# Adding up the scaled parts of a chunk with eight identity matmuls on TensorE, all input shares first, and the FFN half a chunk later

## The reference, cut to what matters

```python
# x: (32, 32, 256) = batch, time, features; cond: (32, 256) is the first state
# 1. a GRU over 32 time steps (state h: 32 x 256, weights 256 x 768)
gi = x_t @ W_ih + b_ih;  gh = h @ W_hh + b_hh
r = sigmoid(i_r + h_r);  z = sigmoid(i_z + h_z)
n = tanh(i_n + r * h_n); h = (1 - z) * n + z * h
# 2. an FFN over all 1024 states (tokens), a mixture of 128 experts on 8 basis parts of 128
probs = softmax(h @ w_router); top 4 -> topk_w (normed)
basis = silu(h @ w_gate) * (h @ w_up)            # 8 parts of 128
mix   = rows of (a0**2 + a1**2) / sum, per expert
out   = sum over the 4 of topk_w * scale * (mix_sel . basis) @ w_down
out  += silu(h @ sw_gate) * (h @ sw_up) @ sw_down  # the shared expert, 256 wide
# 3. result = x + out
```

## Time and profile before

| what | before |
|---|---|
| median of 3 runs | 151.68 us (151.32 to 153.98) |
| the profiled execution | 151.24 us, span of the trace 149.4 us |
| PE matmuls busy | 136.4 us (91%), 1482 records |
| PE weight loads busy | 99.2 us (66%) |
| DVE / ACT / POOL busy | 110.7 / 68.3 / 66.3 us |
| mean granted TensorE clock | 0.985 of full speed |

### The profile page before, as it was taken

One profiled execution on the slowest core, in us unless ns is written; L12 is line 12 of the kernel. 1 busy time (PEld: TensorE's weight loads), 2 busy tenths in 40 slices (PEclk: granted clock), 3 DMA queues, 4 the chain that ended last, 5 costly groups with the idle time before them and its releaser, 6 DMA issues.

```text
span 149.4 us, 4027 instructions
## 1 busy us (share of the span) xinstructions
PE 136.4 (91%) x1482; PEld 99.2 (66%) x1482; DVE 110.7 (74%) x410; ACT 68.3 (46%) x222; POOL 66.3 (44%) x125
## 2 busy tenths in 40 slices
PE   7939999799973998999999999999999999899991
PEld 5528877576552665866777676767766875588880
DVE  2113668699987499789878987898888789859661
ACT  1303466666436454544544554455544552513830
POOL 2201113477459197149324923481457146556030
PEclk9995999999999999999999999999999999999998
DMA  3999990000000000000000000100010001000102
GB/s 89 346 208 213 383 318 9 7 4 2 0 0 4 0 0 4 0 16 23 4 0 29 11 0 0 37 4 0 2 39 0 0 4 37 0 0 0 35 4 70
DMA packets 5763, 7.12 MB, mean 48 GB/s; under 512 B 880, under 2 KB 4208, under 8 KB 5744
## 3 DMA queue, kind: packets, MB, share of 16 engines
q1 hardware_dynamic: 5324, 6.63, 15.9%
q10 hardware_dynamic: 420, 0.24, 0.6%
HBM read 5.81 MB, written 1.05 MB: 46 GB/s over the span
## 4 chain that ended last, share of the span: by engine, by line
PE 68%; DVE 12%; POOL 6%; DMA 5%; ACT 2%; issue 2%; SPq 2%; DVEq 0%
PE unit L611 29%; PE gates L602 14%; PE down L676 6%; PE unit L581 5%; DMA whh<-in_L_cond_W_hh_dram 5%; PE gates L566 4%; DVE sc_out L848 2%; POOL wlo L341 2%; ACT sc_add L418 2%; POOL dlo_w L348 1%; PE route L541 1%; DVE wlo L868 1%; PE route L623 1%; DVE pre L839 1%; DVE hT L855 1%
## 5 line engine op out<-in xcount | busy, mean ns | idle before, releaser
L611 PE MATMUL unit<-whi,hThi 128*128 128x512 f32 x80 | 33.8, 422 | 3.7 <-POOL wlo L341 3.2
L306 POOL CAST hThi<-hT 128x64 fp32r<-128x64 f32 x32 | 8.9, 279 | 60.1 <-DVE hT L855 59.7
L611 PE MATMUL unit<-whi,hTlo 128*128 128x512 f32 x80 | 31.6, 395 | 0.0
L611 PE MATMUL unit<-wlo,hThi 128*128 128x512 f32 x80 | 31.6, 395 | 0.0
L602 PE MATMUL gates<-whh,hT 128*32 128x192 f32 x512 | 27.9, 336 | 3.7 <-DMA whh<-in_L_cond_W_hh_dram 2.5
L411 ACT ACTIVATE trz<-gates 128x128 f32<-128x128 f32 x32 | 8.9, 278 | 48.4 <-PE gates L602 48.4
L602 PEld LDWEIGHTS gates<-whh,hT 128*32 128x32 f32 x512 | 14.0, 110 | 14.5 <-issue 7.5
L848 DVE TENSOR_TENSOR_SCAN sc_out<-sc_mul,sc_add 128x128 f32<-128x128 f32 x32 | 15.4, 482 | 8.2 <-ACT sc_add L418 8.1
L611 PEld LDWEIGHTS unit<-whi,hThi 128*128 128x128 f32 x80 | 15.1, 188 | 9.5 <-POOL wlo L341 4.0
L611 PEld LDWEIGHTS unit<-whi,hTlo 128*128 128x128 f32 x80 | 15.0, 188 | 3.5
L896 DVE SCALAR_TENSOR_TENSOR p<-th,unit 128x256 f32<-128x256 f32 x40 | 15.9, 410 | 1.5 <-ACT th L439 1.5
(11 more groups left out here) (127 smaller groups left out, 240.4 us busy)
## 6 DMA issues: line engine op xcount, KB each, us to landing
wraw<-in_L_ffn_w_gate_dram SPq DMA_DIRECT2D x2, 512.0 KB, 10.2
wraw<-in_L_ffn_w_up_dram SPq DMA_DIRECT2D x2, 512.0 KB, 11.6
out_dram<-ot SPq DMA_DIRECT2D x7, 128.0 KB
wih<-in_L_cond_W_ih_dram SPq DMA_DIRECT2D x2, 384.0 KB, 4.2
xtok<-in_x_dram SPq DMA_DIRECT2D x4, 192.0 KB, 7.4
whh<-in_L_cond_W_hh_dram SPq DMA_DIRECT2D x1, 512.0 KB, 7.8
whh<-in_L_cond_W_hh_dram SPq DMA_DIRECT2D x1, 256.0 KB, 5.5
wraw<-L_ffn_shared_w_gate_dram SPq DMA_DIRECT2D x1, 256.0 KB, 11.3
```

The lines of the kernel that those rows point to most:

```text
L611: last = pe.matmul(dst, st[:, p % 3, s, :, :].rearrange("p t b -> p (t b)"), w[:, s, :, cols], start=(s == 0 and n == 0), stop=(s == KB - ...
```

## The change

- `add_basis` and `mixed` are gone. `turn_hidden` makes the sum and the transpose together: eight f32 matmuls, each with one scaled part (`qc`) as the stationary operand and the identity as the moving one, accumulate in `turned`. It moves from slot part 2 to part 1. `scale_basis(p, 0)` now also waits until the previous chunk's `turn_hidden` has read `qc`.
- `EARLY` holds all steps from 4 on, so 14 pairs are made, two per step from step 2 to 7. `SKEW` is 4.
- The logits' hi and lo router columns add up in PSUM (four matmuls of 128 columns in place of two of 256), so `lx` is a copy, on ACT. `keys`, `negmax` and `den` go from DVE to ACT, and `hhalf` (`halve`) too, where it stands behind `load_gates` and ahead of the slot. ACT takes `emT` right behind its tanh of n. DVE's `dlo` comes behind `q` in part 2.
- Tokens of a chunk are in (batch, step) order rather than (step, batch): x is loaded and the result stored by one transfer a chunk; `hThi` and `hTlo` are written with a stride of 4 elements, xT is read from PSUM with one.
- SP waits for the first half of `wih` before it issues the other six chunks of x. Between the input shares of steps 0 and 1, 10 further warm-up matmuls are added (and two on the gates' banks).

```diff
-SKEW = 2
-EARLY = [4, 5, 6, 7, 10, 11, 14, 15, 18, 19, 22, 23, 26, 27, 30, 31]
-EARLY_PAIRS = [[0], [1], [2], [3, 4], [5], [6, 7]]
+SKEW = 4
+EARLY = list(range(4, T))
+EARLY_PAIRS = [[0], [1], [2, 3], [4, 5], [6, 7], [8, 9], [10, 11], [12, 13]]
...
         def _(sp):
-            load_x(sp, range(0, 2), 0, 2, ld_xfirst)
+            load_x(sp, 0, 1)
             for s in range(KB):
-                sp.dma_start(wih[:, s, :], pairs(w_ih)[:, s, :]).then_inc(ld_wih, 16)
+                sp.dma_start(wih[:, s, :], pairs(w_ih)[:, s, :]).then_inc(ld_wih[s], 16)
...
-            load_x(sp, range(TC), 2, NC, ld_xrest)
+            sp.wait_ge(ld_wih[0], 16)
+            load_x(sp, 2, NC)
...
                 if part == 0:
                     pool.wait_ge(coef_ready, p + 1)
+                    if p >= 1:
+                        pool.wait_ge(turned_ready, p)
...
-            def add_basis(p):
-                pool.wait_ge(pool_mix, MIX_STEPS * p + 2)
-                pool.tensor_tensor(half[:, :], qc[:, 0:4 * I], qc[:, 4 * I:8 * I], ALU.add).then_inc(pool_mix, 1)
...
+            def halve(t):
+                act.wait_ge(h_ready, t + 1)
+                act.activation(natural(hhalf, slice(0, FJ)), by_block(sc_out, 1), ACT.Copy, scale=0.5)\
+                    .then_inc(hhalf_ready, 1)
...
                 for s in range(KB):
-                    pe.matmul(route[:, LOGITS], hThi[:, p % 3, s, :, :].rearrange("p t b -> p (t b)"),
-                              wrouter[:, s, :, :].rearrange("p a e -> p (a e)"),
-                              start=(s == 0), stop=False, skip_group_check=True)
+                    for a in range(2):
+                        pe.matmul(route[:, LOGITS], hThi[:, p % 3, s, :, :].rearrange("p b t -> p (b t)"),
+                                  wrouter[:, s, a, :], start=(s == 0 and a == 0), stop=False, skip_group_check=True)
...
                 pe.wait_ge(pool_mix, MIX_STEPS * (p + 1))
                 if p >= 1:
                     pe.wait_ge(dlo_ready, p)
-                pe.transpose(turned[:, 0:P], mixed[:, :], ident[:, :])
+                else:
+                    pe.wait_ge(early_ready, NE // 2)
+                for k in range(K):
+                    pe.matmul(turned[:, 0:P], qc[:, I * k:I * (k + 1)], ident[:, :], start=(k == 0), stop=(k == K - 1))
                 pe.transpose(turned[:, P:2 * P], shared[:, p % 2, 0:P], ident[:, :])
...
                     if k == 1:
                         unit(NU * p + 1, [1])
-                        unit(NU * p + 2, range(KB))
+                        if p >= 1:
+                            turn_hidden(p - 1)
+                        unit(NU * p + 2, [0])
                     if k == 2:
                         turn_em(p)
-                        if p >= 1:
-                            turn_hidden(p - 1)
+                        unit(NU * p + 2, [1])
                         unit(NU * p + 3, range(KB))
                         coefficients(p)
...
             turn_x(0, route, 0)
+            keep_warm(6)
+            x_part(0, [0])
             turn_x(1, unit_bank[2], 0)
+            keep_warm(4)
+            x_part(0, [1])
+            x_part(1)
             keep_warm(3)
-            x_part(0)
-            x_part(1)
...
                 elif k == 2:
                     gated_p1(NU * p + 1)
+                    gated_q(NU * p + 1)
                     if p >= 1:
                         lo_turned(p - 1, turned, slice(0, 3), p)
-                    gated_q(NU * p + 1)
                     scale_coefficients(p)
```

More of the change, by code:

```diff
@@ L440, in tanh_gate, with copy_logits, topk_keys, topk_den @@
                     .then_inc(th_ready, 1)
+            def copy_logits(p):
+                act.wait_ge(logits_ready, p + 1)
+                if p >= 1:
+                    act.wait_ge(topk_step, TOPK_STEPS * p)
+                act.activation(lx[:, 0:E], route[:, LOGITS], ACT.Copy).then_inc(lx_ready, 1)
+            def topk_keys(p):
+                act.wait_ge(max_ready, p + 1)
+                act.activation(negmax[:, :], v8[:, 0:1], ACT.Copy, scale=-1.0).then_inc(keys_ready, 1)
+                act.activation(keys[:, 0:TOPK], v8[:, 0:TOPK], ACT.Copy).then_inc(keys_ready, 1)
+            def topk_den(p):
+                act.wait_ge(topk_step, TOPK_STEPS * p + 2)
+                act.activation(den[:, :], exsum[:, :], ACT.Identity, bias=sum4[:, :], scale=EPS).then_inc(den_ready, 1)
             def softmax_exp(p):
-                act.wait_ge(topk_step, TOPK_STEPS * p + 3)
+                act.wait_ge(keys_ready, 2 * p + 2)
                 act.activation(ex[:, :], lx[:, 0:E], ACT.Exp, bias=negmax[:, :], accum_out=exsum[:, :])\
@@ L553, in wait_x, with x_part @@
                     pe.wait_ge(x_turned, c // 2 + 1)
-            def x_part(t):
+            def x_part(t, blocks=range(KB)):
                 g = gates[t % 2]
@@ L561, in x_part @@
                     pe.wait_ge(gates_loaded, t - 1)
-                if t == 0:
-                    pe.wait_ge(ld_wih, 32)
-                for s in range(KB):
+                for s in blocks:
+                    if t == 0:
+                        pe.wait_ge(ld_wih[s], 16)
                     for j in range(NJ):
@@ L641, in unit @@
                             pe.wait_ge(w_lo_pool, LO_POOL.index(i) + 1)
-                if n >= NB and 0 in blocks:
-                    pe.wait_ge(q_ready, n - NB + 1)
+                if 0 in blocks:
+                    if n >= NB:
+                        pe.wait_ge(q_ready, n - NB + 1)
+                    else:
+                        pe.wait_ge(early_ready, 1 + max(i for i in range(NE // 2) if i % len(early_bank) == n))
                 last = three(unit_bank[n % NB][:, :].rearrange("p (g n) -> p g n", g=2), p,
@@ L1012, in slot @@
                         mixing_table(4)
-                    topk_den(p)
                     gated_q(NU * p)
-                    topk_rec(p)
+                    if p >= 2:
+                        residual(p - 2, down)
                     if p == 0:
@@ L1028, in slot @@
                     gated_q(NU * p + 3)
-                    if 1 <= p < LAST - 1:
-                        residual(p - 1, down)
             for c in range(NC):
```

182 lines of the change are left out of this document (84 added, 98 removed).

## The result

The changed kernel takes **161.7 us** (median of 4 runs, 161.5 to 161.8); the kernel before took 152.5 in its runs beside it (4 runs, 151.32 to 153.98). The ratio is 1.063, 95% interval 1.054 to 1.072: **slower**, and inside the forecast range. The profiled execution took 161.7, its span 159.8, 10.4 more than the 149.4 of before.

The account below looks back on a forecast made before the run. PE was taken as the bound: work +12.95, idle removed -5.75, idle added +1.6 and +1.5, start -1.8, together +8.5 us on the profiled execution, giving 159.7 us, range 155.8 to 162.8.

Parts of the forecast that it names:

- Sum on PE: Chunks 0 to 6: eight identity matmuls at 0.22 us replace a 0.11 transpose, +1.65 a chunk, +11.55 us in all.
- Router: Router matmuls on PE: four of 128 columns cost 0.34 us instead of 0.24, +0.10 a chunk, +0.8 in all.
- Chunk in mid-run: Sign of being right: a mid-run chunk takes 14.9 us, or 15.2 with the new wait, against 14.37 before.
- Wait for `dlo`: Ahead of `project` in chunks 1 to 5: PE waits 0.3 us more a chunk, +1.5 us in all.
- Idle removed: From step 1 to the last chunk: PE's 5.9 us of idle time goes, but for 0.16, -5.75 us.
- chunk 0: In the first chunk PE has too few matmuls to fill GRU steps and idles, +1.6 us.
- Start: Before step 1: `whh` lands at 10.1 us, clock at 2.4 GHz, step 1 starts at 13.1, -1.8 us.
- POOL's work falls and nothing comes of it.: Expected sign: POOL's busy time falls by some 17 us without making the kernel faster.
- 3 (0.11 a matmul): Rival, chance 0.08: identity matmuls run at transpose pace, the sum costs 5.4 us, time 153.5, or 152 with a good start.
- 4 (slack on PE): Rival, chance 0.05: added matmuls fill drains between PE's unit matmuls, time 147 to 152 us.
- 1 (1 us a chunk): Rival, chance 0.17: `dlo` or the scan makes PE wait 1 us a chunk, +3.5, time 163 us.
- 2 (no wait): Rival, chance 0.20: `whh` lands at 8.8 us and `dlo` is in time, time 156.5 us.

Follow-up runs that it names:

- Experiment 1: Kernel before with only the sum on PE: eight identity matmuls replace POOL's additions and the transpose; median 162.28 us, ratio 1.064.
- experiment 4: Changed kernel with four of the eight identity matmuls, the other four parts left out of the sum; median 156.38 us, ratio 1.029.
- experiment 5: Changed kernel with eight overwriting transposes in place of the eight accumulating identity matmuls; median 159.43 us.
- experiment 6: Changed kernel with one line moved, so that DVE makes `dlo` ahead of `q` in part 2; median 159.34 us, ratio 1.046.
- experiment 9: Kernel before with POOL's last three `wlo` weight pieces a step earlier; median 150.13 us, ratio 0.981.
- experiment 10: Kernel before with the moves alone: early input shares, FFN two steps later, weight pieces at the change's places; median 151.31 us, ratio 0.997.
- experiment 8: Kernel before with the new start alone: x held behind half of `wih`, 14 more warm-up matmuls; median 150.76 us, ratio 0.986.
- experiment 11: Kernel before with the new start and the earlier `wlo` pieces together; median 150.87 us, ratio 0.984.
- experiment 12: Kernel before with early input shares, later FFN, the new start, and `negmax` and `keys` on ACT; median 151.94 us, ratio 1.001.
- experiment 2: Changed kernel with the sum back on POOL, one transpose, and the turn, `dhi` and `dlo` at their old places; median 157.99 us, ratio 1.028.
- experiment 3: Kernel of experiment 2 without POOL's additions: POOL only scales, and one scaled part is turned; median 153.15 us, ratio 0.989.
- experiment 7: Changed kernel with the halving of the state back on DVE; median 158.63 us, ratio 1.038.

## Why the prediction was right, and where its terms were off

The mechanism was right: the kernel is bound by PE, the change puts 11 to 12 us of matmuls on it and cannot win back as much. Experiment 1 gives +9.9 for the sum alone, experiments 4 and 5 give 0.20 us a matmul, 0.22 where nothing else is near. The total was met (span 157.9 forecast, 159.8 measured) with errors of both signs.

- **Sum on PE, +11.55.** Confirmed where it was read: 8 x 0.22 = 1.78. Net of what it replaces it was 1.56 a chunk in mid-run of experiment 1, not 1.65, and 9.9 in all, since part of it fell into time in which PE had waited.
- **Router, +0.10 a chunk.** Off by a factor of two: 0.59 + 0.22 - 0.43 - 0.17 = 0.21 in the chain. The pair on `hTlo` also went from 0.17 to 0.22, which the forecast left as it was. The two errors cancel in mid-run: 14.37 - 1.30 + 1.56 + 0.21 + 0.09 = 14.93.
- **Chunk in mid-run.** Forecast 14.9 without and 15.2 with the new wait; experiment 6 has 14.94 without it, the changed kernel 15.41 with it.
- **Wait for `dlo`, +0.3 a chunk.** The term of the sum that was mis-sized: 0.5 (2.6 us in five waits, for 1.5). The chain from the state share to the end of `dlo` was forecast at 4.49 and took 112.09 - 107.59 = 4.50. PE's side was too long by 0.14: it was ready 4.06 after the state share (112.14 less the wait of 0.49), not 4.2. A difference of two paths of over 4 us each was the term, and a small error in one doubled it.
- **Idle removed, -5.75, and chunk 0, +1.6.** Up to 39.0 PE idles 0.04 us, no wait for `wlo` is left, chunk 0 idles 1.71. The first logits come at 39.54, forecast about 40.
- **Start, -1.8.** -1.34 in the two profiled executions: `whh` landed at 10.49 instead of 10.1, and step 1 followed at 13.54, at a granted clock of 1.00. The size is near, the mechanism (x held back behind `wih`) is not shown. The larger transfer of `whh` took 7.8, 7.7, 7.2 and 6.5 us in the kernel before and its variants with the old order (before, experiments 1, 9 and 10), and 6.7, 8.7 and 7.8 with x held back (8, 11 and 12). In the changed kernel and its variants, where x also comes in one transfer a chunk, it took 6.2 to 7.3; which part of the change does that wasn't tried. The same for the clock: it fell to 0.5 behind PE's wait of over 2 us for `whh` in the kernel before and in experiment 1, and stayed at 1.00 with the same start in experiment 10, where that wait was 1.1.
- **Last chunk.** The step that was missing. The book adds to its 15.40 us only the sum, the router and the change of type, 1.84; it took 3.22 more. The turn of chunk 6 now waits 0.91 for DVE's `shared`, which comes behind the top-k instructions. In experiment 1, with the old order and the same sum on PE, the last chunk took 159.2 - 142.2 = 17.0, and in experiment 2, with the old order and the sum on POOL, 15.3; here it took 18.6. So about half of the 3.2 is the sum and half the new order and what goes with it.
- **Chunk 6.** 11.06 from its logits to the next, without GRU steps and full of matmuls; 11.87 before (122.13 to 134.00), with the last GRU step in it and the idle 0.89 of the earlier trace rows.
- **"POOL's work falls and nothing comes of it."** True for this change, since PE stays the bound, but true for a reason that I did not see. Experiments 2 and 3 differ only in POOL's additions and by 5.7 us. They cost nothing only as long as PE hides DVE. In experiment 12, where PE has less to do, the instructions that stretch beside them are on the chain (`sc_add` and the scan, 1.8 us together for 0.7); in experiment 10 it is `keys` beside the scaling, which the change keeps, and the scan. No run leaves the additions out there. So the change did take a real load away, at about double its price.
- **The rivals.** 3 (0.11 a matmul) and 4 (slack on PE) are refuted: matmuls 0.22 apart, each costing 0.20 in the time, although weight loads are busy only 70%. The Trainium skill's rule for reading slack from that share (Perfetto Trace Analysis, Identifying the Most-Contended Engine) does not hold for the 4-byte matmuls of this kernel; the measurement decides. 1 (1 us a chunk) and 2 (no wait) lie on both sides of what came.

In the book of PE: busy forecast 149.35, measured 148.9; idle forecast 8.55, measured 10.9. That the busy time agrees so well is in part luck: up to step 1 the warm-up matmuls added 1.7 us that the book did not have, and the first input shares and step 0, no longer at half the clock, gave back 1.5. The 2.4 us between are mainly the waits for `dlo` (+1.1), the start (+0.5) and the last chunk's turn (+0.9).

## What to carry to other kernels

Where the chain is one engine alone for a whole stage, cost a change by that engine's book, start to start, and check the engine's waits at every place that the change reorders, the last round included. Moving work to the bound engine costs its full time there, even when it unloads another; the one cheap gain that is shown here was a wait that needs no work moved (`wlo` a step earlier, 1.6 us in chunk 0). The start shows the other side: two profiled executions that agree with the forecast prove nothing where executions of one kernel differ by as much. And before counting on a less busy bound engine, look at the next one while its neighbour runs: its instructions may not keep the durations that they show alone.

## What the runs showed of the hardware

- DVE instructions that read two SBUF tiles stretch beside POOL's: the scan from 0.42 to 0.92, `sc_add` from 0.27 to 0.80 and 0.93. A copy of 128x4 within SBUF, which reads one tile, stretches too, from 0.29 to 0.88. `m` and `pre`, with an input from PSUM, kept their times (0.22).
- An f32 matmul of 128x128 against the identity costs 0.22 us start to start at a granted clock of 1.00, a transpose of the same tile 0.11.
- Where the chain at the start waits for `whh`, it landed between 9.84 and 11.08 us: at 11.08, 11.01 and 9.84 with the old start (before, experiments 1 and 10), at 10.49, 9.98 and 11.05 with the new one (the changed kernel, experiments 8 and 12). In the profiled executions of the other eight experiments the chain there is PE's own early work, and step 0 comes at 9.90 to 10.82 in experiments 3, 4, 6 and 7, at 11.78 in experiment 9, and at 13.90, 13.88 and 13.93 in experiments 2, 5 and 11. In those last four, 9 included, PE's early matmuls run at about half their later pace up to 11 us and more, at a granted clock that the trace gives as 1.00. That is the size of the spread between runs of one kernel; whether it is all of it wasn't tried.
